# Graph convolutions: the edge ids, slots and weights of two steps in one load from a table in DRAM

## The chip, the cores and the metric

One core of one Trainium2 chip runs the kernel. The metric is the device time of one execution, in microseconds (us). The kernel before took 8839.22 us, the median of three runs (8838.54 to 8855.53).

Each engine has its own queue of instructions: TensorE (PE), VectorE (DVE), ScalarE (ACT), GpSimd (POOL) and SyncE (SP). They meet at semaphores that instructions and landing DMAs raise.

## The reference

A graph has 12500 nodes of 96 features and 400000 edges, sorted by destination. Two blocks follow one another; each adds its result to its input.

```
h  = relu(layernorm(x))
x  = x + L0(h)      # edge messages: gelu(MLP([h[src], attr])) gated, summed by dst; node update; layernorm
h  = relu(layernorm(x))
for W, b, Wr, br in two layers:                       # L1
    msg = norm[:, None] * (h @ W)[src]                # norm = dinv[src] * weight * dinv[dst], self loops added
    xc  = segment_sum(msg, dst) + b
    g   = sigmoid(h @ Wr + br)
    h   = relu((1 - g) * h + g * xc)
out = x + h
```

The change touches the two convolutions of L1 (the loop), and the place where the edge pass of L0 begins.

## The kernel before

The edges are padded to 401408 and cut into 3136 tiles of 128. Eight tiles are a group. All edges of a group go to nodes that lie close together, so that their sum is one window of 64 nodes.

**The order of the program.** The setup makes a table of source features in DRAM. The edge pass of L0 runs over all tiles; beside it, the last 1536 tiles ("sides") are turned into a block adjacency matrix that is kept in DRAM. The node update makes the features of L1 and the first convolution's table. Then convolution 0, its combine, convolution 1, and the output follow.

**A convolution** handles the other 1600 tiles, 200 groups, edge by edge, and the sides by matmuls with the adjacency matrix.

- A *step* is two groups (even steps, j = 0) or four (odd steps, j = 1). There are 67 steps: three lead steps (8 groups), then 16 *units* of four steps (4, 2, 4 and 2 groups, 12 in all).
- POOL gathers, tile by tile, the table rows of a group's 128 sources with an indirect DMA (L1007); the row numbers are `conv_ids`. A group's buffer is free when PE has summed the group six places earlier (`s["seg"]`).
- DVE *spreads* a group: it compares the slots `conv_rel` with a row of 0 to 63 (L1950) and multiplies by the weights `conv_wt` (L1954).
- PE sums a group with eight matmuls of gathered rows and spread slots (L1227, each recorded as two). Between groups it runs the adjacency matmuls: 14 *pieces* a unit, each of 14 matmuls (L1240), from a ring of four buffers that ACT's queue fills. Before the first and the seventh group of a unit stand two pieces, before each other group one.
- DVE adds the sums to `acc` (L1972) and the sides' results (L1988). In 14 of the units it also computes two *mix* halves (L1997 to L2012), the gate of the layer.

**What SP does.** SP's queue issues the small loads of a convolution in program order. For each step there are three: ids from `in_src` (L789), slots from `rel_keep` (L795), weights from `in_weight` (L797), into `hid` (its columns `streams`). `load_step_after` waits until a step's rows have all been gathered, loads the ids of two steps later into the same buffer, waits until the step has been spread (`s["weighted"]`), and loads the slots and weights. Between the steps of a unit SP waits for the mix on DVE and moves its operands (L812 to L817). POOL waits for a step's ids before its gathers, DVE for a step's slots and weights before its first spread; ACT waits for those of the first two steps before it fills the ring.

**Where the slots come from.** `rel_keep` is a table in DRAM, one slot a tile and partition, for two ways of running a convolution: with the sides done by matrix (the first 1600 columns), or, in further passes for inputs that don't fit it, edge by edge with the last 1600 tiles. Just before the edge pass ACT's queue stores `rel` and a constant `never` into it (L1399 to L1401) and then waits for both (`act.wait_ge(s_rel_out, 32)`, L1407). Its next instruction is the first gelu of the edge pass (`gelu`, L1345), on which the whole chain of that pass hangs.

Of the kernel before, what the change touches and what calls it, by code (L numbers as in the profile page):

```python
# [90 lines left out]
STEPS = LEAD_STEPS + UNIT_STEPS * UNITS  # L91
UNIT_SLOTS = [(k, slot) for k in range(LEAD_STEPS, LEAD_STEPS + UNIT_STEPS) for slot in range(STEP_SIZE[k % 2])]
STEPS_OF = [(STEPS + 1) // 2, STEPS // 2]
FANS = UNIT_QUADS * WIDTH
# [77 lines left out]
def build(nc, io):  # L172
    ctx = contextlib.ExitStack()
    with ctx:
# [9 lines left out]
        def dram(name, shape):  # L184
            return nc.dram_tensor(name, shape, F32).ap()
# [15 lines left out]
        rel_keep = dram("rel_keep", [P, 2 * MAIN_TILES])  # L201
# [145 lines left out]
        conv_ids = [streams[:, STEP_TILES * j:STEP_TILES * (j + 1)].bitcast(I32) for j in range(2)]  # L347
        conv_rel = [streams[:, STEP_TILES * j:STEP_TILES * (j + 1)] for j in range(2, 4)]
        conv_wt = [streams[:, STEP_TILES * j:STEP_TILES * (j + 1)] for j in range(4, 6)]
        side_base = streams[0:1, 6 * STEP_TILES:6 * STEP_TILES + UNIT_QUADS].bitcast(I32)  # L350
        side_out = streams[0:D, 6 * STEP_TILES + UNIT_QUADS:6 * STEP_TILES + UNIT_QUADS + FANS]

# [61 lines left out]
        s_rel_out = sem("rel_kept")  # L414
# [40 lines left out]
        s_conv_ids = [sem(f"conv_ids{j}_in") for j in range(2)]  # L455
        s_conv_edges = [sem(f"conv_edges{j}_in") for j in range(2)]
# [178 lines left out]

        def table_chunk(c, k=0, m=TILES_PER_CHUNK):
            return table_sb[:, bass.ds(c * CF + D * k, D * m)]
# [15 lines left out]
        def _(sp):  # L653
# [64 lines left out]
            def load_side_edges(c, done):  # L718
                cols = bass.ds(MAIN_TILES + c * SLICE, SLICE)
                sp.dma_start(prep_i[0][:, :], io["src_side"][:, bass.ds(c * SLICE, SLICE)]).then_inc(s_prep_in, 16)  # L720
# [3 lines left out]
            def keep_side_rel(c, done):  # L724
                wait_apart(sp, s_prep, done * ALL_PREP + ALL_PREP)
                sp.dma_start(rel_keep[:, bass.ds(MAIN_TILES + MASKED + c * SLICE, SLICE)],
                             prep_rel[:, :]).then_inc(s_prep_out, 16)
# [58 lines left out]
            for l in range(2):  # L786

                def load_ids(j, k, late, u=0):
                    sp.dma_start(conv_ids[j][:, 0:GROUP * STEP_SIZE[j]].rearrange("p (g t) -> p g t", t=GROUP),  # L789
                                 io["src"][bass.ds(late * LATE_GROUPS + group_of(k, 0, u), STEP_SIZE[j]), :, :  # L790
                                           ].rearrange("g p t -> p g t")).then_inc(s_conv_ids[j], 16)

                def load_edges(j, k, late, u=0):
                    tile0, width = GROUP * group_of(k, 0, u), GROUP * STEP_SIZE[j]
                    sp.dma_start(conv_rel[j][:, 0:width],  # L795
                                 rel_keep[:, bass.ds(late * MAIN_TILES + tile0, width)]).then_inc(s_conv_edges[j], 16)
                    sp.dma_start(conv_wt[j][:, 0:width],  # L797
                                 io["weight"][:, bass.ds(late * SIDE_TILES + tile0, width)]).then_inc(s_conv_edges[j], 16)
# [20 lines left out]
                def conv_unit(u, n0, u0, h0, late, mix, more, s=cv[l], m=mx):  # L819
# [4 lines left out]
                    for k in range(UNIT_STEPS):  # L824
# [1329 lines left out]
```

## Time and profile before

| what | us |
|---|---|
| median of three runs | 8839.22 |
| the profiled execution, first to last instruction (span) | 10933.0 |
| setup, to the first gelu of the edge pass (0 to 158) | 158 |
| edge pass (158 to 5720) | 5562 |
| node update (5720 to 6010) | 290 |
| convolution 0 (6010 to 8395) | 2385 |
| combine (8395 to 8470) | 75 |
| convolution 1 (8470 to 10856) | 2386 |
| output (10856 to 10933) | 77 |

The profile is of one execution under the hardware profiler; its span is its own time, and it is 1.24 times the median of the runs. The stages are cut at their first and last instructions in the trace. A busy share counts the engine's own instructions, not its waits or DMA issues; "issue" as the end of an idle stretch means that nothing that the profile records was waited for.

### The profile page before, as it was taken

To read this page: it belongs to the slowest core of one execution; us is meant where nothing else is said; L and a number is where in the kernel's file an instruction comes from. 1 tells how busy PE (TensorE), PEld (TensorE's weight loads), DVE (VectorE), ACT (ScalarE), POOL (GpSimd) and SP (SyncE) were. 2 spreads that over 40 slices of the span, in tenths; PEclk is the share of its full clock that TensorE was granted. 3 is DMA by queue.
4 is the path that set the end of the run, shared out by engine and by line. 5 is a ranking of instruction groups with operands and counts; after the bars stand their busy time and mean duration, and the time that the engine had idled before them with its cause. 6 is when DMAs were issued, how large, how long until landed. Compare 5 with 4: busy or idle time off the path is not lost. (4 is left out here: it accounts for less than half of the span.)

```text
span 10933.0 us, 150076 instructions
## 1 busy us (share of the span) xinstructions
PE 8192.3 (75%) x42144; PEld 5220.9 (48%) x42144; DVE 4899.6 (45%) x11836; ACT 2690.1 (25%) x6600; POOL 6435.5 (59%) x6424
## 2 busy tenths in 40 slices
PE   4777777777777777777777578887777577887776
PEld 4555555555555555555555233333334333433333
DVE  7666666666666666666667122222222121222222
ACT  3444444444444444444443000000000000000000
POOL 4555555555555555555554666666664666666663
PEclk7888888888888888888887788888887688888887
DMA  4444444444444444444444456666565465666656
GB/s 147 123 138 131 136 132 136 132 135 132 135 133 135 133 135 135 134 135 133 135 132 134 155 207 220 216 218 214 208 212 198 156 215 206 224 217 210 210 207 207
DMA packets 933049, 1818.03 MB, mean 166 GB/s; under 512 B 277359, under 2 KB 745600, under 8 KB 875312
## 3 DMA queue, kind: packets, MB, share of 16 engines
q10 hardware_dynamic: 65600, 773.65, 18.6%
q1 hardware_dynamic: 615456, 578.39, 16.9%
q0 software_dynamic: 251856, 464.10, 14.8%
q8 instruction: 93, 1.52, 0.1%
q14 instruction: 44, 0.36, 0.0%
HBM read 1361.12 MB, written 454.48 MB: 166 GB/s over the span
## 5 line engine op out<-in xcount | busy, mean ns | idle before, releaser
L962 POOL DMA_INDIRECT hid<-src_table,src_ids x3127 | 3136.7, 1003 | 2510.4 <-ACT msg L1358 1590.2
L1240 PE MATMUL bd<-ring,table_sb 128*96 128x480 f32 x6272 | 2941.6, 614 | 513.3 <-issue 511.7
L1240 PEld LDWEIGHTS bd<-ring,table_sb 128*96 128x96 f32 x6272 | 1071.7, 176 | 2131.6 <-issue 2131.1
L1007 POOL DMA_INDIRECT hid<-conv_table,hid x1596 | 1561.9, 979 | 751.1 <-issue 486.2
L1155 PE MATMUL sg<-hot,msg 128*98 128x64 f32 x6272 | 831.1, 286 | 1115.9 <-ACT msg L1358 1105.2
L1132 PE MATMUL bd<-one_hot_dst,one_hot_src 128*128 128x168 bf16 (+1 forms) x10368 | 1277.0, 274 | 253.5 <-issue 252.3
L1007 POOL DMA_INDIRECT feat_in<-conv_table,hid x1056 | 1026.1, 972 | 545.2 <-issue 324.6
L1155 PEld LDWEIGHTS sg<-hot,msg 128*98 128x98 f32 x6272 | 746.8, 199 | 1252.2 <-issue 1180.0
L1972 DVE TENSOR_TENSOR acc<-acc,sg 96x64 f32 x400 | 87.2, 218 | 2450.0 <-remote 1652.7
L1132 PEld LDWEIGHTS bd<-one_hot_dst,one_hot_src 128*128 128x128 bf16 x10368 | 1007.1, 110 | 299.1 <-issue 284.3
L1367 ACT ACTIVATE blocks<-bd 128x480 f32<-128x480 f32 (+1 forms) x1152 | 658.1, 571 | 1704.7 <-PE bd L1132 811.8
L1709 DVE SCALAR_TENSOR_TENSOR one_hot_src<-iota_lo,side_now 128x384 bf16<-128x384 bf16 x1536 | 933.8, 608 | 0.0
L1358 ACT ACTIVATE msg<-hid,msg 128x96 f32<-128x96 f32 x3136 | 909.8, 363 | 52.7 <-DVE msg L1686 45.8
L1099 PE MATMUL pa<-w_attr,attr 128*128 128x384 f32 x1568 | 820.1, 660 | 57.9 <-DVE hid L1662 37.9
L1345 ACT ACTIVATE hid<-hid 128x768 f32<-128x768 f32 x784 | 656.8, 838 | 281.2 <-DVE hid L1662 230.6
L1465 ACT ACTIVATE buf_b<-pa,mix_b_half 96x448 f32<-96x448 f32 x56 | 35.3, 630 | 2768.6 <-remote 1515.8
L1007 POOL DMA_INDIRECT rows_more<-conv_table,hid x528 | 526.9, 998 | 301.6 <-issue 153.6
L1612 DVE TENSOR_TENSOR acc<-acc,sg 98x64 f32 x392 | 87.1, 222 | 1284.5 <-remote 1253.3
L1099 PE MATMUL pb<-w_attr,attr 128*128 128x384 f32 x1568 | 592.3, 501 | 7.8 <-issue 4.6
L1950 DVE TENSOR_TENSOR conv_hot<-iota_now,hid 128x512 f32<-128x512 f32 x134 | 92.6, 691 | 958.9 <-remote 517.0
L1099 PEld LDWEIGHTS pa<-w_attr,attr 128*128 128x128 f32 x1568 | 396.9, 280 | 262.6 <-issue 151.8
L1479 ACT ACTIVATE hid<-bd,side_flag 96x480 f32<-96x480 f32 x32 | 21.0, 657 | 1958.2 <-PE bd L1240 1126.1
(248 smaller groups left out, 10307.8 us busy)
## 6 DMA issues: line engine op xcount, KB each, us to landing
ring<-adjacency ACTq DMA_DIRECT2D x448, 1680.0 KB
adjacency<-blocks SPq DMA_DIRECT2D x384, 980.0 KB
attr<-in_attr SPq DMA_DIRECT2D x392, 128.0 KB
hid<-src_table,src_ids POOLq DMA_INDIRECT x3127
hid<-conv_table,hid POOLq DMA_INDIRECT x1596
feat_in<-conv_table,hid POOLq DMA_INDIRECT x1056
conv_table<-table_sb SPq DMA_DIRECT2D x28, 336.0 KB, 2.4
feat_half<-feat_keep SPq DMA_DIRECT2D x56, 168.0 KB
```

The costliest lines, as they stand in the source:

```text
L962: pool.indirect_dma_start(out=hid[s][:, t, :], out_offset=None, in_=src_rows, in_offset=bass.IndirectOffsetOnAxis(ap=src_ids[h][:, j:j + 1 ...
L1007: pool.indirect_dma_start(out=conv_g[j][slot][:, t, :], out_offset=None, in_=conv_rows[l], in_offset=bass.IndirectOffsetOnAxis(ap=conv_ids ...
L1099: last = nc.tensor.matmul(attr_ps[s % 2][:, 512 * h:512 * h + 2 * H2], attr[s // 2][:, P * (s % 2):P * (s % 2 + 1)], w_attr[:, 2 * H2 * h: ...
L1132: op = nc.tensor.matmul(out[:, :, bass.ds(places[q][t], FAN)], y_s[q][t][:, k, :], z_s[q][t][:, z0:z0 + FAN * m].rearrange("p (b d) -> p b ...
L1155: op = nc.tensor.matmul(sums[s // 2][0:ACC_ROWS, :], msg[s % 2][:, t, :], hot[s % 2][:, t, :], start=(s % 2 == 0 and t == 0), stop=(s % 2 ...
L1240: op = nc.tensor.matmul(side_ps[w].rearrange("r (o z) -> r o z", o=UNIT_OCTETS), table_sb[:, D * k:D * (k + 1)], ring[slot][:, :, OCTET_FA ...
L1345: nc.scalar.activation(flat, flat, ACT.Gelu).then_inc(s_gelu, 1)
L1358: op = nc.scalar.activation(m[:, t, 0:D], hid[s][:, t, 0:D], ACT.Copy, scale=m[:, t, GATE_ROW:GATE_ROW + 1])
L1367: nc.scalar.activation(blocks[h][:, first:first + m, WIDTH * q:WIDTH * (q + 1)], part_bank[i % BANKS][:, 0:WIDTH * m].rearrange("p (b w) - ...
L1709: v.scalar_tensor_tensor(out=y_s[q][t][:, :, :], in0=iota_lo[:, :].unsqueeze(1).to_broadcast([P, 3, P]), scalar=side_now[:, 0, QUAD * q + ...
L1950: v.tensor_tensor(conv_s[j][slot], iota_now[:, :].unsqueeze(1).to_broadcast([P, GROUP, WINDOW]), conv_rel[j][:, cols].unsqueeze(2).to_broa ...
L1972: v.tensor_tensor(window, window, sg[j][0:D, WINDOW * slot:WINDOW * (slot + 1)], ALU.add).then_inc(s["acc"], 1)
```

## The change

A new table `edge_keep` in DRAM takes the place of `rel_keep`: for each tile and partition the slot, the weight and the source id, for the same 2 x 1600 columns. ACT's queue fills it where it stored `rel` before: six stores of which four are new (two of `weight` from SBUF, two of the ids from the input in DRAM to DRAM), and it waits for all six.

A *half* is a pair of steps: half 0 is step 0 alone, half q is steps 2q - 1 and 2q, six groups or 48 tiles. One DMA loads its three streams into `conv_in[q % 2]`. SP waits once for it, until PE has summed the last group of the half before last (`s["seg"]`), and loads. POOL and DVE wait at the first step of a half alone. `side_base` moves to another buffer; the side edges' ids are read from the new input `src_cols`.

On SP, at the top of the loop over the units of convolution 0 with mix, before (`in_src`, `rel_keep` and `in_weight` are the three sources, ISA and REGISTER_ALU rows hold the waits):

```order
L812 DMA feat_half<-feat_keep0 96x448
L813 DMA buf_h0<-dinv_rows 96x448
L561 ISA
L789 ISA
L789 DMA hid<-in_src 128x4x8
L561 ISA
L795 ISA
L795 DMA hid<-rel_keep 128x32
L797 ISA
L797 DMA hid<-in_weight 128x32
L561 ISA
L561 REGISTER_ALU
```

These are the first step's three loads, of four such places in a unit. The same place now, as far as the unit's second load:

```order
L823 DMA feat_half<-feat_keep0 96x448
L824 DMA buf_h0<-dinv_rows 96x448
L565 ISA
L810 ISA
L810 DMA hid<-edge_keep 128x3x48
L565 REGISTER_ALU
L827 DMA mix_scale0<-buf_h0 96x448
L828 DMA mix_add0<-buf_b0 96x448
...
L565 ISA
L810 ISA
L810 DMA hid<-edge_keep 128x3x48
```

Twelve loads in a unit became two, one on either side of the mix half's stores and loads.

On ACT, where the edge pass begins, before (`L1345` is the first gelu):

```order
L547 DMA buf_h<-h_src 128x672 x2
L1399 DMA rel_keep<-rel 128x1600
L1401 DMA rel_keep<-never 128x64
L581 UNCONDITIONAL_BRANCH
L581 ISA
L1345 ACTIVATE hid<-hid 128x768
```

In the same place now (`L1355` is that gelu):

```order
L551 DMA buf_h<-h_src 128x672 x2
L1409 DMA edge_keep<-rel 128x1600
L1413 DMA edge_keep<-weight 128x1600
L1414 DMA edge_keep<-in_src_cols 128x1600
L1413 DMA edge_keep<-weight 128x1600
L1414 DMA edge_keep<-in_src_cols 128x1600
L1416 DMA edge_keep<-never 128x64
L585 UNCONDITIONAL_BRANCH
L585 ISA
L1355 ACTIVATE hid<-hid 128x768
```

Four stores stand ahead of the last one and of the wait for all.

The diff, cut to what matters:

```diff
+HALF_STEPS = 2
+HALF_TILES = PAIR_GROUPS * GROUP
+STREAMS = 3
...
-        rel_keep = dram("rel_keep", [P, 2 * MAIN_TILES])
+        edge_keep = dram("edge_keep", [P, STREAMS, 2 * MAIN_TILES])
...
+        conv_in = [streams[:, STREAMS * HALF_TILES * b:STREAMS * HALF_TILES * (b + 1)]
+                   .rearrange("p (f t) -> p f t", f=STREAMS) for b in range(2)]
...
+        def half_of(k):
+            return (k + 1) // HALF_STEPS
+        def starts_half(k):
+            return k == 0 or k % HALF_STEPS == 1
+        def half_loaded(k, c0, u=0):
+            return c0 * (16 * LOADS_OF) + (half_of(k) // 2 + u) * 16 + 16
...
-                def load_step_after(j, m, k, n0, late, u=0, s=cv[l]):
-                    for slot in range(STEP_SIZE[j]):
-                        wait_apart(sp, s_rows[j][slot], rows_gathered(m, j, slot))
-                    load_ids(j, k + 2, late, u)
-                    wait_apart(sp, s["weighted"], n0 + group_of(k, STEP_SIZE[j], u))
-                    load_edges(j, k + 2, late, u)
+                def load_half(q, late, u=0):
+                    k, width = max(0, HALF_STEPS * q - 1), HALF_TILES if q else GROUP * STEP_SIZE[0]
+                    sp.dma_start(conv_in[q % 2][:, :, HALF_TILES - width:HALF_TILES],
+                                 edge_keep[:, :, bass.ds(late * MAIN_TILES + GROUP * group_of(k, 0, u), width)]
+                                 ).then_inc(s_conv_in[q % 2], 16)
+                def load_half_after(q, n0, late, u=0, s=cv[l]):
+                    wait_apart(sp, s["seg"], n0 + (group_of(HALF_STEPS * q, STEP_SIZE[0], u) + SEG_CREDIT))
+                    load_half(q + 2, late, u)
...
-            act.dma_start(rel_keep[:, 0:MAIN_TILES], rel[:, 0:MAIN_TILES]).then_inc(s_rel_out, 16)
+            act.dma_start(edge_keep[:, 0, 0:MAIN_TILES], rel[:, 0:MAIN_TILES]).then_inc(s_edges_kept, 16)
+            for late in range(2):
+                main = slice(late * MAIN_TILES, (late + 1) * MAIN_TILES)
+                tiles_of = slice(late * SIDE_TILES, late * SIDE_TILES + MAIN_TILES)
+                act.dma_start(edge_keep[:, 1, main], weight[:, tiles_of]).then_inc(s_edges_kept, 16)
+                act.dma_start(edge_keep[:, 2, main].bitcast(I32), io["src_cols"][:, tiles_of]).then_inc(s_edges_kept, 16)
...
-            act.wait_ge(s_rel_out, 32)
+            act.wait_ge(s_edges_kept, 16 * 6)
```

## Rows read from the trace of the kernel before

**Rows 1.** The page's first part: span; busy us, share, instructions of each engine.

```profile
span 10933.0 us, 150076 instructions
PE 8192.3 (75%) x42144; PEld 5220.9 (48%) x42144; DVE 4899.6 (45%) x11836; ACT 2690.1 (25%) x6600; POOL 6435.5 (59%) x6424
```

**Rows 2.** Busy time by stage: setup, edge pass, convolutions 0 and 1.

```profile
core 0: us, PE busy (x) PEld busy (x) DVE busy (x) ACT busy (x) POOL busy (x), PEclk, DMA share, GB/s
0.00:158.00 158.00, 88.63 (x526) 81.77 (x526) 104.21 (x174) 68.92 (x147) 55.43 (x40) 0.86 0.60 203
158.00:5720.00 5562.00, 4170.04 (x27422) 3146.49 (x27423) 3503.10 (x8734) 2439.29 (x6152) 3096.72 (x3088) 0.85 0.43 132
6010.00:8395.00 2385.00, 1806.82 (x6448) 891.76 (x6448) 493.68 (x1156) 28.16 (x44) 1557.34 (x1590) 0.84 0.58 204
8470.00:10856.00 2386.00, 1839.30 (x6448) 886.13 (x6448) 493.49 (x1155) 28.16 (x44) 1557.64 (x1590) 0.84 0.58 204
```

**Rows 3.** Waits in both convolutions: waiter, releaser, total us, times, longest us.

```profile
POOL hid L1007 <- issue: 486.2, 1516, 15.7
...
POOL hid L1007 <- remote: 234.5, 69, 5.9
...
DVE conv_hot L1950 <- DMA hid<-in_weight: 188.4, 20, 22.4
...
PE sg L1227 <- DMA hid<-conv_table,hid: 51.5, 6, 15.8
...
DVE conv_hot L1950 <- DMA hid<-rel_keep: 33.6, 1, 33.6
...
PE sg L1227 <- DMA feat_in<-conv_table,hid: 16.7, 3, 7.1
...
POOL hid L1007 <- DMA hid<-in_src: 9.9, 2, 9.6
...
PEld sg L1227 <- DVE conv_hot L1954: 0.2, 1, 0.2
```

**Rows 4.** One group of convolution 0 on DVE: start, us, instruction, idle before.

```profile
7293.92 0.69 DVE L1950 TENSOR_TENSOR conv_hot<-iota_now,hid 128x512 f32<-128x512 f32 x1 [17.12 <-remote]
```

**Rows 5.** The same group's first and last gathers on POOL.

```profile
7294.70 1.47 POOL L1007 DMA_INDIRECT feat_in<-conv_table,hid  x1 [3.41 <-PE sg L1227]
7296.47 0.95 POOL L1007 DMA_INDIRECT feat_in<-conv_table,hid  x1 [0.30 <-issue]
...
7303.98 0.95 POOL L1007 DMA_INDIRECT feat_in<-conv_table,hid  x1 [0.30 <-issue]
```

**Rows 6.** PE around the same group's sum, two pieces before it, and the next group.

```profile
7337.23 1.49 PE L1227 MATMUL sg<-x_c,hid 128*96 128x64 f32 x16
7338.56 11.46 PE L1240 MATMUL bd<-ring,table_sb 128*96 128x480 f32 x28
7349.86 0.22 PE L1227 MATMUL sg<-conv_hot,feat_in 128*96 128x64 f32 x1
...
7355.13 5.80 PE L1240 MATMUL bd<-ring,table_sb 128*96 128x480 f32 x14
7360.77 1.49 PE L1227 MATMUL sg<-buf_h,feat_in 128*96 128x64 f32 x16
```

**Rows 7.** ACT where the edge pass begins.

```profile
149.21 0.44 ACTq L1399 DMA_DIRECT2D rel_keep<-rel  x1
149.69 0.44 ACTq L1401 DMA_DIRECT2D rel_keep<-never  x1
157.90 1.57 ACT L1345 ACTIVATE hid<-hid 128x768 f32<-128x768 f32 x2 [36.91 <-DMA rel_keep<-never]
```

**Rows 8.** POOL's next gather there.

```profile
162.47 1.06 POOL L962 DMA_INDIRECT hid<-src_table,src_ids  x1 [20.09 <-ACT msg L1358]
```

**Rows 9.** DMA issues: count, KB each, median us from issue to landing.

```profile
src_table<-s_c SPq DMA_DIRECT2D x7, 672.0 KB, 3.0
...
x_keep<-x_c SPq DMA_DIRECT2D x14, 336.0 KB, 2.2
...
setup_edges<-in_dst SPq DMA_DIRECT2D x1, 1568.0 KB, 6.2
...
hid<-in_src SPq DMA_DIRECT2D x68, 8.0 KB
...
hid<-in_src SPq DMA_DIRECT2D x66, 16.0 KB
...
rel_keep<-rel ACTq DMA_DIRECT2D x1, 800.0 KB, 7.8
```

**Rows 10.** SP's first load of convolution 0.

```profile
6006.97 0.40 SPq L789 DMA_DIRECT2D hid<-in_src  x1
```

**Rows 11.** POOL's first gather of convolution 0.

```profile
6011.14 1.29 POOL L1007 DMA_INDIRECT hid<-conv_table,hid  x1 [15.71 <-issue]
```

More of the change, by code:

```diff
@@ L91 @@
 STEPS = LEAD_STEPS + UNIT_STEPS * UNITS
+HALF_STEPS = 2
+HALF_TILES = PAIR_GROUPS * GROUP
+STREAMS = 3
+HALF_LOADS = (STEPS + 1) // HALF_STEPS
+LOADS_OF = (HALF_LOADS + 1) // 2
 UNIT_SLOTS = [(k, slot) for k in range(LEAD_STEPS, LEAD_STEPS + UNIT_STEPS) for slot in range(STEP_SIZE[k % 2])]
 STEPS_OF = [(STEPS + 1) // 2, STEPS // 2]
+assert HALF_LOADS == 2 * LOADS_OF
 FANS = UNIT_QUADS * WIDTH
@@ L346, in build @@
         streams = hid_all[:, 3 * GROUP * D:]
[L347 to L351, printed above, removed]
+        conv_in = [streams[:, STREAMS * HALF_TILES * b:STREAMS * HALF_TILES * (b + 1)]
+                   .rearrange("p (f t) -> p f t", f=STREAMS) for b in range(2)]
+        side_out = streams[0:D, 2 * STREAMS * HALF_TILES:2 * STREAMS * HALF_TILES + FANS]
+        side_base = feat_space[0][0:1, GROUP * D:GROUP * D + UNIT_QUADS].bitcast(I32)
         side_diag = prod[:, :, :].rearrange("p t f -> p (t f)")[:, 0:P]
@@ L454, in build @@
                 "base", "eaten", "out", "added")} for l in range(2)]
-        s_conv_ids = [sem(f"conv_ids{j}_in") for j in range(2)]
-        s_conv_edges = [sem(f"conv_edges{j}_in") for j in range(2)]
+        s_conv_in = [sem(f"conv_edges{b}_in") for b in range(2)]
         s_rows = [[sem(f"conv_rows{j}{slot}") for slot in range(STEP_SIZE[j])] for j in range(2)]
@@ L634, in rows_gathered, with stream_cols @@
             return m * (16 * GROUP) + 16 * (GROUP - CONV_SPARED[group_of(j, slot)])
+        def half_of(k):
[4 more added lines that the diff above has]
+            return c0 * (16 * LOADS_OF) + (half_of(k) // 2 + u) * 16 + 16
+        def stream_cols(k, slot):
+            first = 0 if k % 2 else STEP_SIZE[1]
+            return slice(GROUP * (first + slot), GROUP * (first + slot + 1))
         def table_chunk(c, k=0, m=TILES_PER_CHUNK):
@@ L823, in conv_unit @@
                         load_mix_half(u * 2)
-                    for k in range(UNIT_STEPS):
-                        if more or k < UNIT_STEPS - 2:
-                            step = k + LEAD_STEPS
-                            load_step_after(step % 2, u * 2 + step // 2, step, n0, late, u)
-                        if mix and k == 1:
+                    for i in range(2):
+                        if more:
+                            load_half_after(half_of(LEAD_STEPS) + i, n0, late, u)
+                        if mix and i == 0:
                             wait_apart(sp, m["done"], h0 + u * 2 + 2)
@@ L851, in _ @@
                     h0 = sp.snap(conv_pass(p, l, passes) * HALVES)
-                    for k in range(2):
-                        load_ids(k, k, late)
-                        load_edges(k, k, late)
+                    for q in range(2):
+                        load_half(q, late)
                     sp.wait_ge(s_dinv_out, 16)
@@ L857, in _ @@
                         sp.wait_ge((s_feat_new, s_kept_out)[l][q], 16 * (CHUNKS // 2))
-                    for k in range(LEAD_STEPS):
-                        load_step_after(k % 2, k // 2, k, n0, late)
+                    for q in range(2):
+                        load_half_after(q, n0, late)
                     with sp.Fori(0, MIX_UNITS) as u:
@@ L1488, in _ @@
                     u0, h0 = act.snap(p * UNITS), act.snap(cp * HALVES)
-                    for j in range(2):
-                        wait_apart(act, s_conv_ids[j], cp * (16 * STEPS_OF[j]) + 16)
-                        wait_apart(act, s_conv_edges[j], cp * (32 * STEPS_OF[j]) + 32)
+                    for k in range(2):
+                        wait_apart(act, s_conv_in[k], half_loaded(k, cp))
                     for i in range(RING):
@@ L2021, in conv_unit @@
                             if more or at < UNIT_STEPS - 1:
-                                spread_step(k + 1, (k + 1) % 2, u * 2 + (k + 1) // 2, slot, n0, c0, u)
+                                spread_step(k + 1, slot, n0, c0, u)
                             add_group(k - 1, (k - 1) % 2, slot, n0, late, done, u)
@@ L2041, in _ @@
                         for slot in range(STEP_SIZE[(k + 1) % 2]):
-                            spread_step(k + 1, (k + 1) % 2, (k + 1) // 2, slot, n0, c0)
+                            spread_step(k + 1, slot, n0, c0)
                         for slot in range(STEP_SIZE[(k - 1) % 2] if k > 0 else 0):
```

53 lines of the change are left out of this document (21 added, 32 removed).

## The prediction

> **What bounds the kernel now.** I read the stages first, then the waits of the convolutions, then single groups in the timeline. The page's head gives the span, 10933.0 us [rows 1]; the median of the runs is 8839.2, so the profiled execution is 1.24 times as long, and terms that I take from it as waits may be up to that much too large. The stages [rows 2] show two convolutions of 2385 and 2386 us, 4771 of the 10933. In each PE is busy for 1807 to 1839 us and POOL for 1557.
>
> POOL's busy time is not all that it needs. A gather takes 0.95 us and the next one begins 0.30 us later with nothing waited for [rows 5], so 1590 gathers cost 1590 x 1.25 = 1988 us of the 2385. PE at its best pace needs 5.7 us a piece (11.46 us for two) and about 1.3 us more a group (from the sum's start at 7337.23 to the piece's at 7338.56) [rows 6]. That is 14 x 5.7 + 12 x 1.3 = 95 us a unit, against 96 x 1.25 = 120 us on POOL. In the profiled execution PE is nevertheless the later one: the group that was spread at 7293.92 [rows 4] and gathered from 7294.70 to 7304.93 [rows 5] was summed at 7349.86 [rows 6], 45 us after its last gather. PE loses time in stretches with no recorded cause, and POOL is then held by the credit of six groups. Without the profiler I expect less of this and POOL's pace to decide: 2 x 1988 us in the convolutions. So two regimes are possible, PE first or POOL first, and the change has to be priced in both.
>
> The loads that the change replaces are not late in either. POOL waited for ids twice, 9.9 us in all, at the starts of the convolutions [rows 3]. DVE waited for slots and weights 21 times, 188.4 + 33.6 = 222 us [rows 3], but what DVE does with them is early: the only wait of PE for a spread is one of 0.2 us [rows 3].
>
> **The change part by part.** *Fewer loads.* The count of ids loads is 68 + 66 = 134 [rows 9], three streams make 402; now there are 34 halves a convolution, 68 in all. The 334 that go, and SP's waits for rows and spreads, are issued by SP, which nobody waits for except as above. I take 0 for them. The work that hides them is PE's store of groups: 45 us in the profiled regime. In POOL's regime the ids of a step were asked for when the step two before it had landed, one whole step (2 or 4 groups, 20 or 40 us at 10 us a group) ahead of their use, against 4.2 us from SP's first issue to POOL's first gather [rows 10, 11]. If the cover were gone on DVE's side it would cost the 222 us; on PE's side the row says 0.2.
>
> *The new wait.* A half is now asked for when PE has summed the last group of the half before last. Behind the waiting instruction on SP stand the mix stores and loads and the side bases. The mix load has to reach PE after the seventh sum of the unit, and SP is released by the sixth; two pieces and a sum lie between, 11.46 + 1.5 = 13 us [rows 6], for one load, two stores and two loads on SP. DVE's mix itself is the later condition, before and now, so 0. POOL may begin the first group of the new half when PE has summed one group more, and between these two sums stand the same two pieces: 13 us, against 4.2 for a load. So where POOL follows PE it still waits for the sum, not for the load. Where POOL is the slower one it arrives six groups, 60 us, after it left the old half's last group, and the sum of that group comes some 10 us after its gathers: 60 - 10 - 4 leaves over 40 us. I take 0, with 0 below (a wait can't gain) and the price of the rival below above.
>
> *The starts of the convolutions.* The first load carries three streams where the ids went alone. Two starts, each 4.2 us from issue to first gather [rows 10, 11]; a few tenths either way, bounded by one more issue slot of 0.4 us: plus or minus 1 us in all. 0.
>
> *The four new stores.* These stand on the path. ACT sat idle for 36.91 us and was released by the landing of the last store of the table, at 157.90 [rows 7]; POOL's next gather, DVE and PE hung on ACT there [rows 8], and nothing later gives the time back, since each iteration starts with the one before it. The four stores have 800 KB each. For such a store in a row of others the trace has sizes to compare: 336 KB land in 2.2 us, 672 KB in 3.0, 1568 KB in 6.2 [rows 9]. So a further 336 KB cost 0.8 us, or 2.4 us for each 800 KB; by the larger pair (1568 - 336) KB cost 4.0 us, 2.6 us each. Four cost 9.5 to 10.4. The lower bound is the later issue of the last store alone, 4 x 0.48 us = 2 (149.21 to 149.69 [rows 7]), if all transfers ran beside each other. The upper bound is 4 x 7.8 = 31, if each took what the lone 800 KB store took [rows 9]. Two of the four go from DRAM to DRAM, which no row shows. I take 10, near the two pairs, because the 7.8 us holds the two loads that were issued before that store.
>
> *The sum* is made against the profiled execution: 10933 + 0 + 0 + 0 + 10 = 10943. A store's landing is not stretched the way PE's pace is, so I add the same 10 to the median: 8839 + 10 = 8849.
>
> A rule of the Trainium skill speaks for more. Its page "DMA: Bandwidth & Descriptors", section "Bandwidth", says to batch DMAs and that those under 64 KB are dominated by their descriptors; section "Anatomy of one DMA — SWDGE (gpsimd) path" gives each DMA a fixed 2.0 us. The loads here are 8 and 16 KB, and 334 of them go: by that rule, an estimate, 668 us if they stood one after another on the path, or 8181 us. The trace disagrees as far as the path goes: POOL's two waits of 9.9 us in all are what these loads ended.
>
> **The rivals.**
>
> *Faster: the gathered rows come sooner.* 334 DMAs fewer share the 16 DMA engines (busy share 0.58 [rows 2]) with the gathers. PE waited for gathered rows for 51.5 + 16.7 = 68 us [rows 3]. If all of that went, 68 / 1.24 = 55 us: 8849 - 55 = 8794. For it: in POOL's regime PE waits for every group's landing, so that the landing of the last group counts. Against it: these waits fall at nine places, mostly where a convolution begins, and a gather's 1.25 us on POOL is not shortened by an earlier landing.
>
> *Faster: SP's queue is itself a bound.* An issue takes SP 0.40 us [rows 10]; 334 fewer are 134 us, and if SP's queue set the pace of the convolutions that would come off: 8849 - 134 = 8715. Against it: what SP's loads feed was waited for as little as told above. The batching rule of the Trainium skill, page "DMA: Bandwidth & Descriptors", section "Bandwidth", would speak for this rival, and its figure is the 8181 us above.
>
> *Slower: the loads are late for the gathers.* Place: the first group of each half from half 2 on, 32 a convolution, 64 in all. The load can't be asked for before the sum, and decides from the point at which it lands later than 13 us after it, when POOL is free to gather the next half. SP's issues are slow at times, and behind ring transfers a load may take long. If each were 2 us late: 64 x 2 = 128 us, 8849 + 128 = 8977. Against it: 4.2 us measured against 13, and PE's store of 45 us in the one regime, over 40 us of time in the other.
>
> *Slower: the stores go one by one.* 31 us at the front, 8870. For it: the lone 7.8 us, and DRAM to DRAM has no row. Against it: 1568 KB in 6.2.
>
> *The change doesn't do what it says.* If a half's wait were met later than I read it, POOL's gathers would show it as waits for the new load; that is the rival of the late loads.
>
> **How the numbers follow.** Forecast 0.63 (8849, its own range 8838 to 8860); gathers sooner 0.14; SP's queue 0.02; loads late 0.07; stores one by one 0.14. A measurement of this kernel can tell about 0.2%, 17.7 us, from no change: 8821.5 to 8856.9. Faster is 0.14 + 0.02 = 0.16; slower is 0.07 + 0.14 = 0.21; the rest, 0.63, is the same. The range of 8 in 10 goes from the gain of the first rival, 8794, to a little above the stores one by one, 8875.
>
> **What would show it.** In the profile of the changed kernel the first gelu of the edge pass should start about 10 us later than 157.90, released by the last store into the new table; 2 us or 31 us would give the bounds. POOL should show no wait for the new load but at the two starts of the convolutions, and DVE's 222 us of waits for slots and weights should be gone without the convolutions' 2385 us becoming shorter. PE's waits for spreads should stay near 0. The prediction is wrong if the convolutions change by more than 10 us each, or if gathers wait for the load table.

## The result and the profile after

The changed kernel took 8863.7 us (median of 12 runs, 8851.1 to 8870.4) against 8847.2 for the kernel before: ratio 1.0017, interval 1.0009 to 1.0025, so 15 us slower (8 to 22). Eleven further runs beside the kernel before gave 1.0018 (1.0009 to 1.0027). The forecast was 8849, no change, with the range 8794 to 8875.

The profiled execution of the changed kernel has a span of 8867.8 us, like its runs; that of the kernel before was much longer than its own [rows 1]. The two can't be subtracted stage by stage. So the kernel before was profiled once more (run `before_again`, span 8830.7), and rows of before are read from that one below.

The page's first part, answering to [rows 1]: span, then busy us, share and instructions of each engine.

```profile
span 8867.8 us, 148170 instructions
PE 7397.9 (83%) x42144; PEld 4775.7 (54%) x42144; DVE 4925.0 (56%) x11836; ACT 2718.7 (31%) x6600; POOL 6525.5 (74%) x6424
```

The same instructions stand on every engine that computes; of the 2065 us by which the span is shorter than in [rows 1], PE was busy for 794 and idle for the rest.

The start of the edge pass on ACT, first of the kernel before (second profile), then of the changed kernel; start, duration, instruction, idle before and its releaser. They answer to [rows 7].

```profile
147.74 0.88 ACTq L547 DMA_DIRECT2D buf_h<-h_src  x2
148.66 0.44 ACTq L1399 DMA_DIRECT2D rel_keep<-rel  x1
149.14 0.44 ACTq L1401 DMA_DIRECT2D rel_keep<-never  x1
156.95 1.58 ACT L1345 ACTIVATE hid<-hid 128x768 f32<-128x768 f32 x2 [36.53 <-DMA rel_keep<-never]
```

```profile
150.02 0.88 ACTq L551 DMA_DIRECT2D buf_h<-h_src  x2
150.95 0.44 ACTq L1409 DMA_DIRECT2D edge_keep<-rel  x1
151.42 0.47 ACTq L1413 DMA_DIRECT2D edge_keep<-weight  x1
151.92 0.86 ACTq L1414 DMA_DIRECT2D edge_keep<-in_src_cols  x1
152.81 0.99 ACTq L1413 DMA_DIRECT2D edge_keep<-weight  x1
153.84 0.85 ACTq L1414 DMA_DIRECT2D edge_keep<-in_src_cols  x1
154.72 0.75 ACTq L1416 DMA_DIRECT2D edge_keep<-never  x1
167.43 0.84 ACT L1355 ACTIVATE hid<-hid 128x768 f32<-128x768 f32 x1 [44.78 <-DMA edge_keep<-never]
```

The moment at which ACT gets to these issues differs by up to 2 us from one execution to the next, so the stores are priced from the first load's issue to the first gelu: 156.95 - 147.74 = 9.21 us before, 167.43 - 150.02 = 17.41 now. The four stores cost 8.2 us there, and the releaser is still the last store, as forecast.

The stages, answering to [rows 2]: us, busy time and count of PE, PEld, DVE, ACT, POOL, granted clock, DMA share, GB/s. The first two rows are the convolutions of before (second profile), the next fence those of the changed kernel.

```profile
4606.00:6635.00 2029.00, 1710.95 (x6432) 854.13 (x6432) 491.88 (x1154) 27.93 (x44) 1544.01 (x1590) 0.91 0.70 239
6718.00:8746.00 2028.00, 1711.88 (x6432) 856.62 (x6432) 492.40 (x1154) 28.13 (x44) 1543.58 (x1590) 0.91 0.70 240
```

```profile
4639.00:6670.00 2031.00, 1720.90 (x6430) 859.79 (x6431) 493.54 (x1153) 27.46 (x43) 1546.67 (x1590) 0.91 0.69 239
6752.00:8786.00 2034.00, 1701.71 (x6429) 857.29 (x6430) 494.47 (x1154) 27.47 (x43) 1548.72 (x1590) 0.92 0.69 239
```

A convolution lasts from POOL's first gather to its last, 2029 and 2028 us before, 2031 and 2034 now, where the first profile had 2385. POOL's busy time is up by 2.7 and 5.1 us for the same 1590 gathers, which is all by which the convolutions are longer.

The waits in the convolutions answer to [rows 3]: waiter, releaser, total us, times, longest us; the first fence is of before (second profile), the second of the changed kernel.

```profile
DVE conv_hot L1950 <- DMA hid<-in_weight: 2624.4, 121, 41.8
...
PEld sg L1227 <- DVE buf_b L1954: 26.0, 3, 16.3
...
POOL hid L1007 <- DMA hid<-in_src: 17.2, 25, 9.9
```

```profile
DVE conv_hot L1966 <- PE sg L1237: 557.2, 68, 12.6
...
POOL hid L1016 <- issue: 509.2, 1583, 16.8
...
PEld sg L1237 <- DVE buf_b L1970: 22.7, 19, 1.9
...
DVE conv_hot L1966 <- DMA hid<-edge_keep: 9.9, 2, 6.1
...
POOL hid L1016 <- PE sg L1237: 4.0, 13, 0.3
```

In an execution of the usual length DVE waited 2624 us for slots and weights, twelve times what the first profile showed; now 9.9, and it waits for sums instead. The convolutions did not become shorter by that. POOL waits for sums 4.0 us in all before its gathers into hid; the 509 us of "issue" are its 0.30 us between gathers and one start of a convolution. Of its 25 waits for ids in the kernel before, one of 9.9 us is such a start, and each of the other 24 is no longer than the 0.30 us that stand before every gather. PE's largest sum of waits for a spread is 26.0 us before and 22.7 now; POOL, which sets the pace, is not held by them.

### The profile page after: what moved, and what is told of

It is laid out like the page before. It is cut to its first block, busy times and chain, and to the rows that moved or that the text cites. A ratio compares the mean times of both kernels' runs of the same rounds, so it can differ in the third digit from the quotient of the medians.

```text
span 8867.8 us, 148170 instructions
## 1 busy us (share of the span) xinstructions
PE 7397.9 (83%) x42144; PEld 4775.7 (54%) x42144; DVE 4925.0 (56%) x11836; ACT 2718.7 (31%) x6600; POOL 6525.5 (74%) x6424
## 4 chain that ended last, share of the span: by engine, by line
POOL 51%; issue 24%; DMA 8%; DVE 7%; PE 6%; ACT 2%; DVEq 1%; POOLq 1%; ACTq 0%; SPq 0%
POOL hid L1016 17%; POOL hid L971 16%; POOL feat_in L1016 11%; DMA hid<-src_table,src_ids 6%; POOL rows_more L1016 6%; DVE hid L1676 2%; DVE one_hot_src L1723 1%; ACT msg L1368 1%; PE bd L1142 1%; PE pb L1109 1%; PE pa L1109 1%; DVE prod L1685 1%; PE sg L1165 1%; POOLq L565 1%; DVE one_hot_dst L1722 1%
## 5 line engine op out<-in xcount | busy, mean ns | idle before, releaser
L971 POOL DMA_INDIRECT hid<-src_table,src_ids x3127 | 3246.3, 1038 | 1027.5 <-issue 905.4
L1250 PE MATMUL bd<-ring,table_sb 128*96 128x480 f32 x6272 | 2716.5, 589 | 0.0
L1142 PE MATMUL bd<-one_hot_dst,one_hot_src 128*128 128x168 bf16 (+1 forms) x10368 | 1139.2, 264 | 0.0
L1109 PE MATMUL pb<-w_attr,attr 128*128 128x384 f32 x1568 | 666.2, 552 | 403.4 <-DVE hid L1676 403.0
L1355 ACT ACTIVATE hid<-hid 128x768 f32<-128x768 f32 x784 | 660.1, 842 | 938.2 <-DVE hid L1676 892.5
L1109 PE MATMUL pa<-w_attr,attr 128*128 128x384 f32 x1568 | 629.1, 525 | 167.0 <-DVE hid L1676 146.2
L1165 PE MATMUL sg<-hot,msg 128*98 128x64 f32 x6272 | 679.3, 253 | 67.6 <-ACT msg L1368 67.6
L1165 PEld LDWEIGHTS sg<-hot,msg 128*98 128x98 f32 x6272 | 637.3, 174 | 80.5 <-DVE acc L1626 47.4
L1676 DVE TENSOR_TENSOR hid<-pb,hid 128x768 f32<-128x768 f32 x392 | 373.5, 953 | 463.8 <-DMA hid<-src_table,src_ids 463.4
L1109 PEld LDWEIGHTS pb<-w_attr,attr 128*128 128x128 f32 x1568 | 286.4, 203 | 575.9 <-DVE hid L1676 447.5
L1722 DVE TENSOR_SCALAR one_hot_dst<-iota_z,side_now 128x688 bf16<-128x688 f16 x1152 | 503.8, 437 | 0.0
```

Of the source, the lines that this page charges most:

```text
L971: pool.indirect_dma_start(out=hid[s][:, t, :], out_offset=None, in_=src_rows, in_offset=bass.IndirectOffsetOnAxis(ap=src_ids[h][:, j:j + 1 ...
L1109: last = nc.tensor.matmul(attr_ps[s % 2][:, 512 * h:512 * h + 2 * H2], attr[s // 2][:, P * (s % 2):P * (s % 2 + 1)], w_attr[:, 2 * H2 * h: ...
L1142: op = nc.tensor.matmul(out[:, :, bass.ds(places[q][t], FAN)], y_s[q][t][:, k, :], z_s[q][t][:, z0:z0 + FAN * m].rearrange("p (b d) -> p b ...
L1165: op = nc.tensor.matmul(sums[s // 2][0:ACC_ROWS, :], msg[s % 2][:, t, :], hot[s % 2][:, t, :], start=(s % 2 == 0 and t == 0), stop=(s % 2 ...
L1250: op = nc.tensor.matmul(side_ps[w].rearrange("r (o z) -> r o z", o=UNIT_OCTETS), table_sb[:, D * k:D * (k + 1)], ring[slot][:, :, OCTET_FA ...
L1355: nc.scalar.activation(flat, flat, ACT.Gelu).then_inc(s_gelu, 1)
```

## The experiments

Two theories stood after the result. Front: the four stores cost 8 us ahead of the first gelu, and the rest is measurement. Convolution: something in the convolutions costs a few us as well.

**1. The kernel before again** (no edit).

> The kernel before, unchanged, profiled and timed again against itself. Both theories expect a ratio of 1.0000 within 0.0008 (7 us). Its profile, if it is free of the stretches in which SP and PE lost time without a recorded cause, says where the 15 us of the changed kernel (8863.7 against 8847.2) stand. Front theory (four stores delay the first gelu, the convolutions are untouched): never's store lands about 0.7 us after rel's, where the changed kernel has 8.3 us (158.93 to 167.23), the first gelu starts 7.5 to 9.5 us earlier than 167.43, and each convolution lasts from first gather to last sum what it lasts in the changed kernel, 2034.4 and 2036.3 us, within 2. Convolution theory (halves loaded at once and later cost a little at each of 68 loads): the convolutions are 3 us or more shorter each here.

Ratio 1.0000 (0.9991 to 1.0009). The front came out as expected, 9.21 us against 17.41; the convolutions were 2028.6 and 2027.8 us (first gather's start to last gather's end) against 2031.2 and 2033.0: 2.6 and 5.2 us apart, where the front theory allowed 2 and the convolution theory wanted 3 or more.

**2. The four stores not waited for.**

```diff
-            act.wait_ge(s_edges_kept, 16 * 6)
+            act.wait_ge(s_edges_kept, 16 * 2)
...
-            dve.wait_ge(s_edges_kept, 16 * 6)
+            dve.wait_ge(s_edges_kept, 16 * 2)
+            dve.wait_ge(s_streams_kept, 16 * 4)
```

The four new stores are issued behind the two old ones, on `s_streams_kept`.

> The changed kernel with its four new stores issued behind the two old ones and on a semaphore of their own, which DVE alone waits for before the convolutions; ACT waits for the two old stores only. Front theory: ACT's wait ends with never's store as in the kernel before, first gelu 7.5 us earlier than 167.43 in the trace, time 8863.7 - 7.5 = 8856 or less, down to the 8847 of the kernel before. Convolution theory: unchanged, 8864, or at most 4 us less. Batching theory (334 fewer loads are worth something once the stores are off the path): below the kernel before, under 8840.

Ratio 1.0004 (0.9995 to 1.0013), some 11 us under the changed kernel; from load to gelu 9.5 us. The front theory's main part holds. No gain over the kernel before shows, so the fewer loads are worth nothing that these runs can tell.

**3. The four stores alone, in the kernel before.**

```diff
+            for late in range(2):
+                act.dma_start(unread[:, 1, main], weight[:, tiles_of]).then_inc(s_rel_out, 16)
+                act.dma_start(unread[:, 2, main].bitcast(I32), io["src_cols"][:, tiles_of]).then_inc(s_rel_out, 16)
...
-            act.wait_ge(s_rel_out, 32)
+            act.wait_ge(s_rel_out, 16 * 6)
```

> The kernel before with the same four stores of 800 KB added between its two, into a table that nothing reads, and waited for by ACT and DVE as in the changed kernel; its convolutions keep the loads of before. Front theory: never's store lands 7.5 us later behind rel's than in the kernel before, time 8847 + 7.5 = 8855, up to 8862 if the whole difference of the change comes from here. Convolution theory: the kernel before's 8847, within 4.

Ratio 1.0006 (0.9997 to 1.0015), 5 us, medians 8 us apart; from load to gelu 17.6 us, as in the changed kernel. The stores are part of the 15 us and, by this run, not all of it.

**4. No wait at the front, then no store at the front.** First ACT's wait alone was moved to the end of its first iteration; then the issues of the stores too, in the changed kernel and in the kernel before. The edit is that of `stores_later`, shortened.

```diff
             def prepared(c, done):
...
+                if is_at(c, 0):
+                    act.dma_start(...)                    # all stores
+                else:
+                    act.wait_ge(s_edges_kept, 16 * 6)
...
-            act.wait_ge(s_edges_kept, 16 * 6)
             edge_pass(act, rounds, edges, ...)
```

> The changed kernel with ACT's wait for all six stores moved from ahead of the edge pass to the end of its first iteration, where ACT first waits for the prepared side edges. Front theory: the first gelu starts as soon as DVE has added the first rows, which in the changed kernel is at about 150.5 instead of 167.43, so 15 us or a little more come off: 8864 - 15 = 8849, and this is 8 us better than with the two old stores waited for. Convolution theory: the same 15 us come off as well, but then the kernel before, which waits 7 us at that place itself, would still be ahead: it would have to be equal to or faster than this one. If other engines are late at that place instead (POOL's gathers were 27.9 us behind ACT), less than 10 us come off.

> The changed kernel with all six stores issued by ACT at the end of its first iteration of the edge pass and waited for at the end of the second (the inputs take one round, so each store is made once). Moving the wait alone left the issues of six stores, 0.5 to 0.95 us each, ahead of the first gelu (155.27). Front theory: the first gelu starts 1 us after ACT's second load of h_src is issued instead of 17, so 16 us less than the changed kernel if nothing else is late there, and 5 us of it come back if ACT's issues hold up the second iteration: 8848 to 8853 where the changed kernel has 8864; level with or 5 us under the kernel before. Convolution theory: 6 us slower than the kernel before with its two stores moved the same way.

> The kernel before with its two stores moved to the end of the first iteration in the same way; its convolutions are those of before. Front theory: 8 us less than the kernel before, ratio 0.9991, first gelu 1 us after the second load of h_src is issued; the changed kernel with its stores moved has the same time within 4 us. Convolution theory: 6 us faster than the changed kernel with its stores moved.

With the wait alone moved, ACT at the start of the edge pass:

```profile
149.88 0.88 ACTq L551 DMA_DIRECT2D buf_h<-h_src  x2
...
154.39 0.67 ACTq L1416 DMA_DIRECT2D edge_keep<-never  x1
155.27 1.58 ACT L1355 ACTIVATE hid<-hid 128x768 f32<-128x768 f32 x2 [32.78 <-issue]
```

The gelu now stood behind ACT's own six issues: 5.4 us after the load, not the 1 us or less expected. Ratio 1.0002 (0.9993 to 1.0011); this run's expectation of beating the stores unwaited by 8 us was a miss. With the stores made later, the changed kernel and the kernel before:

```profile
149.61 0.88 ACTq L551 DMA_DIRECT2D buf_h<-h_src  x2
150.70 1.58 ACT L1355 ACTIVATE hid<-hid 128x768 f32<-128x768 f32 x2 [28.55 <-DVE hid L1678]
```

```profile
148.85 0.88 ACTq L547 DMA_DIRECT2D buf_h<-h_src  x2
149.94 1.58 ACT L1345 ACTIVATE hid<-hid 128x768 f32<-128x768 f32 x2 [28.37 <-DVE hid L1664]
```

Both fronts take 1.1 us, and DVE's rows release ACT. The ratios are 1.0003 (0.9994 to 1.0012) and 0.9992 (0.9983 to 1.0001). The second is the fastest kernel of the study, 7 us under the kernel before, at the edge of what can be told. The first is not: 10 us lie between two kernels that differ in the loads of the convolutions (and in which stores ACT issues in its first iteration).

**5. The changed kernel again** (no edit).

> The changed kernel unchanged, timed and profiled once more. Front theory alone: 8 us (the stores' own 7.8 us and half a microsecond of issue) above the kernel before, ratio 1.0009; both convolutions between 2026 and 2032 us from first gather to last gather's end, as in the kernel before (2025.8 to 2028.7 in the profiles so far). Convolution theory (each convolution is some 3 us longer because POOL's gathers meet DVE's work at other moments): ratio 1.0016, convolutions 2030 to 2034 us.

Ratio 1.0018 (1.0009 to 1.0027), convolutions 2031.8 and 2036.0 us: on the side of the convolution theory, the second convolution 2 us over its range too.

**6. Three loads a half** (on the kernel of experiment 2).

```diff
-                    sp.dma_start(conv_in[q % 2][:, :, ...], edge_keep[:, :, ...]).then_inc(s_conv_in[q % 2], 16)
+                    for f in range(STREAMS):
+                        sp.dma_start(conv_in[q % 2][:, f, ...], edge_keep[:, f, cols]).then_inc(s_conv_in[q % 2], 16)
```

> The changed kernel with its four new stores off the wait (as in the run with stores unwaited, 1.0004 of the kernel before), and each half fetched by three loads, one for each stream, 204 loads instead of 68. Theory that loads off the path cost nothing: the same time as with one load, within 5 us, no wait of POOL for the table but at the starts of the convolutions. Batching theory: 136 more loads of 2 us each on the path, 272 us slower. A middle way, an issue on SP of 0.4 us each: 54 us slower.

Ratio 1.0013 (1.0004 to 1.0022), 8 us over experiment 2 with an uncertainty of 11; POOL waited for no load. The 272 us of the batching theory and the 54 us of SP's issues are excluded; whether it is 0 or 8 is not.

**7. What POOL's gathers cost.** One gather in eight left out; and DVE's spreads made twice.

```diff
-                    for t in range(spared, GROUP):
+                    for t in range(spared, GROUP - (k >= LEAD_STEPS)):
```

```diff
                     v.tensor_tensor(conv_s[j][slot], ..., ALU.is_equal).then_inc(s["hot"], 1)
+                    v.tensor_tensor(conv_s[j][slot], ..., ALU.mult).then_inc(s["once"], 1)
+                    v.tensor_tensor(conv_s[j][slot], ..., ALU.is_equal).then_inc(s["again"], 1)
                     v.tensor_tensor(conv_s[j][slot], ..., ALU.mult).then_inc(s["weighted"], 1)
```

> The changed kernel with one gather in eight left out of every group of the convolutions' units (192 groups a convolution, 384 gathers in all; the eighth row stays what was there before). If POOL's gathers set the pace of the convolutions: 384 times 1.278 us, the mean from start to start, 490 us less, 8861 - 490 = 8371; a unit takes POOL 107 us then, still over PE's 95. If PE or the loads set it: 0 to 50 us less.

> The changed kernel, with DVE making each spread of the convolutions twice over (compare, weight, compare, weight; the same values): 800 more instructions of 0.69 us, 555 us of DVE's time, off the path, since spreads are ready several groups before PE wants them. Theory that only waits count: 0, within 8 us of 8861. Theory that DVE's work stretches POOL's gathers: in the changed kernel's profile the two convolutions hold 94 us of stretch and 980 us of DVE's busy time, 0.096 us a us, so 555 us more cost about 53 us, 30 to 80 with the kinds of work taken apart: 8914.

The convolutions by stage, columns as above, first with one gather in eight left out, then with the spreads made twice:

```profile
4618.00:6412.00 1794.00, 1644.87 (x6432) 817.36 (x6432) 494.40 (x1154) 27.59 (x44) 1367.41 (x1398) 0.96 0.75 265
6494.00:8289.00 1795.00, 1638.61 (x6432) 815.73 (x6432) 493.78 (x1153) 27.71 (x44) 1368.59 (x1398) 0.96 0.74 265
```

```profile
4625.00:6702.00 2077.00, 1722.27 (x6432) 864.15 (x6432) 768.77 (x1554) 28.15 (x44) 1592.39 (x1590) 0.91 0.66 234
6785.00:8862.00 2077.00, 1718.90 (x6432) 862.67 (x6432) 770.25 (x1553) 28.17 (x44) 1592.39 (x1590) 0.91 0.66 234
```

384 gathers less took the ratio from 1.0017 to 0.9472 (0.9458 to 0.9487), 482 us against the 490 expected: POOL's gathers set the pace. Twice the spreads gave 1.0118 (1.0103 to 1.0134), 89 us more than the changed kernel. DVE is busy for 770 of 2077 us there, yet POOL's busy time rose by 89 us (3184.8 against 3095.4): all of the loss lies in gathers that became longer. The expectation, 53 with 30 to 80, was too low.

**8. Where the spreads fall.** The changed kernel's spreads held until the rows of the step two before had landed; and one load a step from the table, asked for when the kernel before asked (both on the front of `stores_later`).

```diff
+                    if slot == 0 and k >= 2:
+                        for before in range(STEP_SIZE[j]):
+                            dve.wait_ge(s_rows[j][before], rows_gathered(u * 2 + (k - 2) // 2, j, before))
```

```diff
+                def load_step_after(k, n0, late, u=0, s=cv[l]):
+                    for slot in range(STEP_SIZE[k % 2]):
+                        wait_apart(sp, s_rows[k % 2][slot], rows_gathered(u * 2 + k // 2, k % 2, slot))
+                    wait_apart(sp, s["weighted"], n0 + group_of(k, STEP_SIZE[k % 2], u))
+                    load_step(k + 2, late, u)
```

> The changed kernel with its stores made later (1.0003 of the kernel before), in which DVE also waits, before it spreads a step, until the rows of the step two before it have landed; that is the moment from which the kernel before asked for that step's slots, so the spreads move to about where they are in the kernel before. What is to be explained: the three pairs with equal fronts (8.0 us of stores apart) leave 3.5, 10 and 10 us for the convolutions, and POOL's gathers there take 84.7 to 97.2 us more than 0.944 us each in the changed kernels' profiles, 81.5 to 86.1 in those with the old loads. Moment theory (the gathers are stretched by DVE's work beside them, and the spreads now fall at a worse place): the convolutions go back to 2026 to 2029 us, excess 81 to 86, time 8 us less than with the stores made later, 0.9994 of the kernel before. Placement theory (the table's columns or the load itself do it): no change, 1.0003 and excess 90 or more. If the 8 us were chance, also no change.

> One part of the change alone: the table of three streams with one load from it for each step (134 loads instead of 68), asked for when the kernel before asked (rows of the step two before landed, and its spread made), on the front of the run with stores made later (1.0003). The spreads then start where they do in the kernel before, a load after the landing. Moment theory (where DVE's work falls beside the gathers decides the stretch): stretch 81 to 87 us as with the old loads, convolutions 2026 to 2029 us, 0.9993 of the kernel before. Table theory (the table's load or the place of its columns costs the 8 us, whenever it is asked for): stretch 90 or more, 1.0003. Batching theory (each load on the path costs its issue, 0.4 us): 66 more loads, 26 us slower than with the stores made later, 1.0033.

The first gave 1.0009 (1.0000 to 1.0018), convolutions of 2039 and 2037 us, and a stretch (POOL's busy time above 0.944 us a gather) of 105 us, where 81 to 86 were expected: the moment of the spreads matters, but this moment is worse, not the one of before. The second gave 0.9998 (0.9989 to 1.0007), 2031.7 and 2029.9 us, stretch 91: between the two theories, so it settles neither. Its 66 additional loads cost nothing that can be told. What the traces of these two runs show of the cause stands in the next section.

## Why the prediction came out as it did

**What bounds the kernel: right.** Of the two regimes only POOL's exists outside the first profile. A unit takes 122 us against the forecast's 120, and leaving gathers out takes their time off almost in full. That POOL's pace would decide was expected, not shown: the only trace at hand had PE as the later one.

**Fewer loads, 0: right.** With the stores off the wait, 334 loads fewer are worth nothing that can be told (1.0004), and 136 more cost at most 19 us. The rival of SP's queue is refuted here: nothing that decides waits for these loads. The batching rule of the Trainium skill (page "DMA: Bandwidth & Descriptors", section "Bandwidth") brought no time here either. The 8181 us were worked out with the 2.0 us of that page's section "Anatomy of one DMA — SWDGE (gpsimd) path", which is stated for DMAs issued on GpSimd; these loads were issued by SP.

**The new wait, 0 with over 40 us of time: right.** A half of the changed kernel, its issue on SP and, in the second fence, POOL's first gather from it:

```profile
6492.81 0.58 SPq L810 DMA_DIRECT2D hid<-edge_keep  x1
```

```profile
6548.84 0.94 POOL L1016 DMA_INDIRECT feat_in<-conv_table,hid  x1 [0.30 <-issue]
```

56 us lie between; over all halves but each convolution's first two the least is 52. The rival of the late loads, and with it the 8977, is gone. So is that of the sooner rows: PE waits for rows, but POOL's pace, not the landing, sets the time (experiment 7).

**The starts of the convolutions, 0 with 1 us either way: right.** From SP's first load to POOL's first gather 5.3 and 3.3 us (4633.74 to 4639.05, 6749.57 to 6752.84) against 4.2 [rows 10, 11].

**The four stores, +10: right in place and mechanism, a little large.** They cost 8.2 us (8.1 and 8.4 in the profiles of experiments 5 and 3), 2.05 us each where I took 2.4 to 2.6 from [rows 9]. The 2.4 was a slip: 0.8 us for 336 KB are 1.9 us for 800 KB, so the rows gave 7.6 to 10.4 for four, and the measured 8.2 lies between. The lone store's 7.8 us and the 31 us made of it are refuted. By the trace the landings follow each other by 2.2, 2.1, 1.9 and 1.5 us, so DRAM to DRAM is no dearer than out of SBUF.

**The step that failed: the convolutions come to 0.** Three pairs of kernels with equal fronts put the new loads at 0.4 (experiment 2 against before), 1.1 (the changed kernel against experiment 3) and 1.1 (the two with stores later) thousandths over the old: 8 us in the mean, with an uncertainty of 6 to 7. With the stores' 8 that is the 15 measured. I had priced a gather at a constant 0.95 us and 0.30 of spacing. Its own row stood in [rows 5]: the first gather there took 1.47 us; it began at 7294.70, while DVE multiplied that group by its weights:

```profile
7294.65 0.69 DVE L1954 TENSOR_TENSOR conv_hot<-conv_hot,hid 128x512 f32<-128x512 f32 x1
```

The second profile of the kernel before shows it plainly, DVE and POOL:

```profile
5705.24 0.94 POOL L1007 DMA_INDIRECT hid<-conv_table,hid  x1 [0.30 <-issue]
...
5706.43 0.69 DVE L1950 TENSOR_TENSOR conv_hot<-iota_now,hid 128x512 f32<-128x512 f32 x1 [35.21 <-DMA hid<-in_weight]
5706.48 1.45 POOL L1007 DMA_INDIRECT hid<-conv_table,hid  x1 [0.30 <-issue]
...
5707.15 0.69 DVE L1954 TENSOR_TENSOR conv_hot<-conv_hot,hid 128x512 f32<-128x512 f32 x1
...
5708.23 0.95 POOL L1007 DMA_INDIRECT hid<-conv_table,hid  x1 [0.30 <-issue]
```

The gather that began with 0.64 us of the compare still to run took 0.5 us longer than its neighbours. In the changed kernel's convolutions 520 of the 3180 gathers begin while DVE runs a spread or a mix instruction with all its inputs in SBUF. They hold all of the stretch, 93.8 of 93.7 us; the other 2660 come to -0.1.

The stretch is 81.5, 83.8 and 86.1 us in three profiles with the old loads (113.1 in the long first one) and 84.7 to 97.2 (mean 91.8) in five with the new (100.2 with three loads a half). That DVE's work beside the gathers costs POOL time is shown by experiment 7; which work makes the 8 us, the traces tell. The part of gathers that begin in a spread is much the same in both, 68.6 to 73.7 and 63.4 to 72.5. The part of those that begin in a mix instruction is not: 11.5 us in each of the three old, 20.2 to 23.0 in the five new. Of the 56 mix halves about 25 have moved by 0.30 us against the gathers. Before (second profile) and after, a gather, the second mix instruction, the fourth and the gather that begins in it:

```profile
5598.61 0.98 POOL L1007 DMA_INDIRECT feat_in<-conv_table,hid  x1 [0.30 <-issue]
5599.39 0.61 DVE L2001 TENSOR_TENSOR buf_b<-pa,buf_h 96x448 f32<-96x448 f32 x1
...
5600.58 0.61 DVE L2004 TENSOR_TENSOR buf_h<-buf_b,buf_h 96x448 f32<-96x448 f32 x1
5601.15 0.94 POOL L1007 DMA_INDIRECT feat_in<-conv_table,hid  x1 [0.30 <-issue]
```

```profile
5627.15 0.94 POOL L1016 DMA_INDIRECT hid<-conv_table,hid  x1 [0.30 <-issue]
5628.23 0.60 DVE L2011 TENSOR_TENSOR buf_b<-pa,buf_h 96x448 f32<-96x448 f32 x1
...
5629.41 0.61 DVE L2014 TENSOR_TENSOR buf_h<-buf_b,buf_h 96x448 f32<-96x448 f32 x1
5629.65 1.19 POOL L1016 DMA_INDIRECT feat_in<-conv_table,hid  x1 [0.30 <-issue]
```

The second mix instruction starts 0.78 us after a gather before and 1.08 now, and the gather that finds the fourth one running is held by 0.25 us instead of 0. Gathers that begin in that fourth instruction hold 2.5 to 3.2 us in the old profiles and 9.4 to 11.1 in the new, most of the difference. So an edit that only moves DVE's work is not free, although nobody waits for it, and here it is the mix that counts, not the spreads. Experiment 8 bears this out in part: both of its edits, with the changed kernel's table and buffers, put the mix back (0.78 us, 10.5 and 11.7 us of stretch), so neither the table's load nor the place of its columns makes that part. Their total did not fall back because gathers that begin in a spread rose to 89.0 and 79.7 us. Open is what moves the mix: its first instruction takes 0.62 us in those 25 halves, where it takes 0.39 to 0.49 in the kernel before, and no run shows why.

**The number.** 8849 stood on the median of three runs, 8839.2. On that of twelve, 8847.2, the same sum gives 8857, and the measured 8863.7 is 7 us above it: the convolutions' 8 us, less the 2 by which the stores' 10 was too large. It lies outside the forecast's own 8838 to 8860 and inside the wide range. The sign "convolutions change by more than 10 us each" was set against the 2385 us of the first profile and would have fired, by over 300 us; against the second profile they changed by 2.6 and 5.2.

## What to carry to other kernels

Find the engine that no one keeps waiting, and price an edit first by what it does to that engine's own instructions: a wait of 2624 us on another engine was worth nothing, and work of a third engine beside the deciding one cost 89 us without a single wait. A table prepared once cost 8 us here because its preparation stood where every engine waits, and saved nothing that could be told when it was moved from there; such preparation is issued after the first work that it would hold up, the issues themselves included. And look at whether the profiled execution is as long as the runs before reading waits from it.

## What the runs showed of the hardware

The gather's stretch beside DVE was not expected: 555 us more of DVE's two-input instructions made POOL's gathers 89 us longer, 0.16 us a us. The profiles give it almost exactly. Of the 520 gathers named above, 493 are longer than 0.944 us by what is left of DVE's running instruction when they begin, less 0.126 us (not at all where less is left), to within 0.01 us. Of the other 27, 20 begin within 0.05 us of DVE's start and are not held, and five, 0.66 us longer, are held by the next DVE instruction too, which follows 0.1 us after the gather's start. A DVE instruction that begins 0.2 us or more after the gather does not lengthen it: 58 gathers of the changed kernel have only such a compare beside them, and none is over 0.01 us longer. Nor does one with an input in PSUM: 43 gathers begin while the mix product of L2011 runs (`pa` is in PSUM), with 0.43 us of it left in the mean, and none is over 0.01 us longer.

The Trainium skill, page "SBUF — State Buffer", section "SBUF: two separate sides", has a rule that fits: DVE and GpSimd share one pair of ports under an exclusive lock, which a DVE instruction with two inputs in SBUF takes only against a GpSimd instruction that reads SBUF; whichever starts first keeps it for its whole instruction, and the other blocks. The gather reads its row numbers from SBUF, and the trace agrees in that it is held until DVE's instruction ends, and in that an input in PSUM takes the effect away. In the other direction the trace differs: a gather does not keep a spread waiting for the whole of its time. The multiplication at 5707.15 above begins 0.67 us into the gather of 5706.48 and takes its usual 0.69 us.

The first profile's 10933.0 us against 8830.7 in the second, same kernel: one execution under the profiler was a quarter longer than another, and in it a wait of 2624 us was one of 222 and PE was later than POOL. Why, no run shows.

ACT's issues of stores of 800 KB took 0.44 to 0.99 us each, and five of them with one of 32 KB in a row held up the engine's next instruction by some 4 us without any wait (5.4 us from load to gelu against 1.1).
